# Softmax attention: one transposed head copied on ScalarE between two exponentials, one head divided on GpSimd

## The reference, cut to what matters

```
q, k = rope(q), rope(k)
dots = einsum('bhqd,bhkd->bhqk', q, k) * SCALE
attn = softmax(dots, axis=-1)
out  = einsum('bhqk,bhkd->bhqd', attn, v) @ w_out
```

## Time and profile before

| what | value |
|---|---|
| median of the runs | 1453.45 us |
| the profiled execution's own time | 1453.37 us |
| its span | 1451.5 us |
| busy share of the span: TensorE (matmul), VectorE, ScalarE, GpSimd | 90%, 71%, 54%, 36% |
| granted TensorE clock, mean of the span | 0.938 |
| share of the chain that ended last: TensorE, VectorE, "issue", ScalarE, GpSimd | 60%, 16%, 9%, 9%, 4% |

### The profile page before, as it was taken

How to read it: one execution, slowest core, us unless ns; L and a number is a source line. 1 busy time by engine, 2 the same in 40 slices (tenths; PEclk the granted TensorE clock), 3 DMA queues, 4 the chain that set the end, 5 groups by cost and what they waited for, 6 DMA issues and landing times.

```text
span 1451.5 us, 30211 instructions
## 1 busy us (share of the span) xinstructions
PE 1308.4 (90%) x9370; PEld 982.7 (68%) x9370; DVE 1025.2 (71%) x2849; ACT 785.3 (54%) x2420; POOL 520.9 (36%) x697
## 2 busy tenths in 40 slices
PE   4999999978888887699999999999999996799997
PEld 2777777753444343577777777777777775799997
DVE  5555555546887788677777777777787764688886
ACT  2232333312223222398888888888888886444442
POOL 3221211123455456544444434444444431111111
PEclk9999999978787777799999999999999998899999
DMA  8000000000000000000000000000000000000000
GB/s 255 1 1 1 0 0 0 0 1 1 1 0 0 0 0 0 1 1 2 2 1 2 1 0 0 0 0 0 0 0 0 1 1 1 1 8 14 11 11 16
DMA packets 14270, 12.22 MB, mean 8 GB/s; under 512 B 1764, under 2 KB 12536, under 8 KB 13944
## 3 DMA queue, kind: packets, MB, share of 16 engines
q1 hardware_dynamic: 14200, 11.33, 2.6%
HBM read 9.23 MB, written 2.10 MB: 8 GB/s over the span
## 4 chain that ended last, share of the span: by engine, by line
PE 60%; DVE 16%; issue 9%; ACT 9%; POOL 4%; DVEq 0%; ACTq 0%; POOLq 0%
PE bank L757 10%; PE bank L939 9%; PE bank L167 8%; PE bank L528 7%; PE bank L477 6%; PE bank L1019 6%; ACT work L956 5%; PE bank L1032 5%; DVE work L948 3%; PE bank L990 3%; ACT work L976 2%; DVE work L1187 1%; DVE work L1179 1%; POOL rstd L342 1%; DVE moe_work L777 1%
## 5 line engine op out<-in xcount | busy, mean ns | idle before, releaser
L956 ACT ACTIVATE work<-bank,work 128x256 f32<-128x256 f32 x512 | 234.8, 485 | 70.6 <-DVE work L948 70.6
L948 DVE TENSOR_REDUCE work<-bank 128x2 f32<-128x512 f32 x256 | 159.0, 684 | 133.3 <-PE bank L939 133.3
L757 PE MATMUL bank<-WrT,xT 128*128 128x512 f32 x256 | 165.0, 792 | 34.1 <-DVE moe_work L777 33.6
L922 POOL TENSOR_TENSOR work<-work 128x512 f32<-128x512 f32 x128 | 160.6, 1277 | 89.0 <-DVE work L912 89.0
L340 POOL TENSOR_SCALAR ve<-mv 128x2 f32<-128x2 f32 x128 | 29.3, 229 | 409.6 <-DVE mv L278 409.6
L976 ACT ACTIVATE work<-work 128x256 f32<-128x256 f32 x384 | 161.4, 534 | 0.0
L970 POOL TENSOR_TENSOR work<-work 128x512 f32<-128x512 f32 x64 | 66.7, 1042 | 252.6 <-DVE work L964 252.6
L486 DVE TENSOR_TENSOR la_work<-bank,tri 128x512 f32<-128x512 f32 x128 | 87.8, 686 | 84.4 <-PE bank L477 84.3
L939 PE MATMUL bank<-work 32*128 32x256 f32 x2048 | 130.4, 391 | 14.2 <-ACT XnT L372 9.8
L990 PE MATMUL bank<-ident,work 128*128 128x128 f32 x1024 | 139.4, 280 | 0.6 <-ACT work L998 0.6
L1019 PE MATMUL bank<-work 128*64 128x256 f32 x1024 | 127.3, 390 | 14.0 <-DVE work L1005 14.0
(11 more groups left out here) (166 smaller groups left out, 2890.1 us busy)
## 6 DMA issues: line engine op xcount, KB each, us to landing
X<-in_x SPq DMA_DIRECT2D x4, 512.0 KB, 5.8
wF<-in_L_ffn_h_w SPq DMA_DIRECT2D x2, 1024.0 KB, 9.6
out<-X SPq DMA_DIRECT2D x16, 128.0 KB, 1.8
w_qkv<-in_L_attn_w_qkv SPq DMA_DIRECT2D x1, 1536.0 KB, 9.4
WrT<-in_L_ffn_Wr SPq DMA_DIRECT2D x1, 1024.0 KB
w_out<-in_L_attn_w_out SPq DMA_DIRECT2D x1, 512.0 KB, 10.5
wF<-in_L_ffn_w_w SPq DMA_DIRECT2D x2, 256.0 KB, 10.3
rope_sin<-in_rope_sin SPq DMA_DIRECT2D x1, 256.0 KB
```

The lines of the kernel that those rows point to most:

```text
L757: ins = nc.tensor.matmul(unit_bank(p, b, t)[:, :], xT[:, p, t * P:(t + 1) * P], WrT[:, b * BLK:(b + 1) * BLK], start=True, stop=True)
L922: nc.gpsimd.tensor_tensor((QT if kind == "q" else KT)[:, p, a, :], rc[:, ru % 2, :], rs_[:, ru % 2, :], ALU.add).then_inc(c_rope, 1)
L948: nc.vector.tensor_reduce(nmax[:, QUAD * a + j, :], SB_[j][:, :].rearrange("p (t k) -> p t k", t=T), AX.X, ALU.max, negate=True).then_inc( ...
L956: ins = nc.scalar.activation(pr[:, a % 2, j, t, :], SB_[j][:, t * LEN:(t + 1) * LEN], ACT.Exp, bias=nmax[:, h, t:t + 1], accum_out=psum_[: ...
```

## The change

ScalarE copies the transposed head 2 of the quad before, between exponentials 0 and 1 of a slot; VectorE copies head 3 alone. The division of head 1 moves from ScalarE to GpSimd, behind that of head 0. The semaphore counts follow. After the last slot ScalarE copies head 2 and VectorE head 3.

```diff
         def sa_turn_tensor(pe, i, a, j):
             n = i * QUADS + a
-            pe.wait_ge(c_pn if j == 0 else c_pna, n + 1 if j == 0 else (QUAD - 1) * n + j)
-            if j < 2:
-                pe.wait_ge(c_ptv, reached(2 * (n - 1) + j + 1))
+            pe.wait_ge(c_pn if j < 2 else c_pna, 2 * n + j % 2 + 1)
+            if j == 1:
+                pe.wait_ge(c_ptv, reached(n))
             else:
-                pe.wait_ge(c_pta, 2 * n + j - 1)
+                pe.wait_ge(c_pta, reached(3 * n + max(j - 1, 0)))
...
         def sa_turn_scalar(act, i, a, j):
-            act.wait_ge(c_v, reached(2 * (n - 1) + 1))
+            act.wait_ge(c_v, reached(2 * (n - 1) + j // 2 + 1))
...
         def sa_pv_tensor(pe, i, p, a, k):
-            pe.wait_ge(c_pta if k == 0 else c_ptv, 2 * n + 2)
+            pe.wait_ge(c_pta, 3 * n + 2 + k)
+            if k == 1:
+                pe.wait_ge(c_ptv, n + 1)
...
@@ gpsimd, sa_step
-                    sa_norm_pool(pool, i, a, 0)
+                    for j in range(2):
+                        sa_norm_pool(pool, i, a, j)
...
@@ vector, sa_step
                     if last:
-                        for j in range(2, 4):
-                            sa_turn_vector(dve, last[0], last[2], j)
+                        sa_turn_vector(dve, last[0], last[2], 3)
...
@@ vector, after the steps
-            for j in range(2, 4):
-                sa_turn_vector(dve, SEQS - 1, QUADS - 1, j)
+            sa_turn_vector(dve, SEQS - 1, QUADS - 1, 3)
...
@@ scalar, sa_step
                     for j in range(QUAD):
                         sa_exp_scalar(act, i, a, j)
-                    for j in range(1, 4):
+                        if j == 0 and last:
+                            sa_turn_scalar(act, last[0], last[2], 2)
+                    for j in range(2, 4):
                         sa_norm_scalar(act, i, a, j)
...
@@ scalar, after the steps
+            sa_turn_scalar(act, SEQS - 1, QUADS - 1, 2)
             sa_pv_scalar(act, SEQS - 1, 1, QUADS - 1)
...
@@ tensor, before the feed-forward network
-            pe.wait_ge(c_pta, 2 * QUADS * SEQS)
-            pe.wait_ge(c_ptv, 2 * QUADS * SEQS)
+            pe.wait_ge(c_pta, 3 * QUADS * SEQS)
+            pe.wait_ge(c_ptv, QUADS * SEQS)
```

## The result

The changed kernel takes 1473.52 us (median of 4 runs, 1472.39 to 1473.96) where the kernel before takes 1453.14 us on the same chip: a ratio of 1.0138, 95% interval 1.012 to 1.0156. It is 20 us slower. The forecast was 1470.5, in a range of 1463 to 1479.

A forecast was written before the change was run, and what follows sets the result against it. TensorE sets the pace, k's start bound by exponential 1. Quads 1 and 2 +14.4, quad 0 +5.2, quad 3 +1.0 and −2.2, sequence 15 −1.2: +17.2 us on 1453.37, forecast 1470.5, range 1463 to 1479.

The forecast's parts named there:

- The copy's price: ScalarE, ahead of exponential 1: copying head 2 delays exponentials 1 to 3 and the k projection by 0.48 us.
- The lower and upper bounds: ScalarE's copy of head 2: at least 0.45 us (pace of half an exponential head), at most 0.61 (no overlap).
- VectorE's saving eaten by exponential 3: VectorE: one copy fewer saves 0.60 us, but the second reciprocals wait for exponential 3, so ropes end 0.25 later.
- the loop's first kind of quad 0: Five loop sequences whose scores after quad 0 wait 0.3 us for L914: +0.25 us each.
- The division costs nothing on GpSimd: GpSimd's second L970, 1.04 us for head 1, ends before the transposes that need it: cost nothing.
- signs of being wrong: k still 0.92 us behind q, transposes waiting for L970's second instruction, or the clock falling in the loop.
- Quad 3: End of quad 3: L372 and the scores come about 0.2 us earlier in eleven slots, −2.2 us.
- Sequence 15: Last sequence, without k projection: −0.12 us a slot, ScalarE's 0.36 once, −0.5 at the end; together −1.2 us.
- The clock: TensorE's clock stays at 1.00; rival: it falls once a sequence, +30 us, 1500 (chance 0.05 together with late GpSimd division).
- sequence 0: The four slots of the first sequence: forecast +1.4 us.
- Faster: Rival: the copy fits in a gap between exponential 1 and k, only the relief remains, −6 us, 1447.5; chance 0.04.
- No change: Rival: TensorE, its work unchanged, absorbs the delay in the waits after quads 0 and 3: 1453 us; chance 0.03.

The follow-up runs named there:

- Experiment 3: The changed kernel with ScalarE's copy of head 2 behind exponential 1 instead of exponential 0: 1457.80 us.
- experiments 6 and 7: First half of P times V moved ahead of the q projection, in the kernel before (1445.34 us) and in the changed kernel (1451.55 us).
- experiment 2: The changed kernel with the division of head 1 back on ScalarE, the copy staying between exponentials 0 and 1: 1481.23 us.
- experiment 1: The kernel before with only the division of head 1 moved from ScalarE to GpSimd: 1447.71 us.
- Experiment 5: The changed kernel with GpSimd dividing heads 0 and 2 and ScalarE heads 1 and 3: 1469.53 us.
- experiment 4: The changed kernel with the first half of P times V moved between the q and k projections on TensorE: 1463.04 us.

## Why the prediction was right, point by point

- **The copy's price, and where it is paid.** Forecast 0.48 us a slot, from the pace of two L998; measured 0.48, with k 1.40 behind q. The lower and upper bounds weren't needed. The Trainium skill, "ScalarE: Activation LUTs", gives an overlap of about 93 ns between neighbours; the copy of 0.59 us at a pace of 0.48 overlaps by 0.11, so the rows of the trace were the better source by a few hundredths. Experiment 3 shows that in quads 1 and 2 the place costs and not the instruction; experiments 6 and 7, with 284.5 us for these quads without the copy and with it, show that this cost exists only as long as TensorE has nothing else to do at that point.
- **VectorE's saving eaten by exponential 3.** Forecast L914 0.25 later in the loop's first kind of quad 0, quad 0 +5.2 us in all; measured +5.1. After the change VectorE waits 0.42 us for exponential 3 ahead of the second reciprocal. Its line in the changed kernel stands in experiment 2. Experiments 3 and 7 leave this term as it is, 128.6 us.
- **The division costs nothing on GpSimd.** Right (experiment 1). One of my signs of being wrong was that L970 would be named as what transposes wait for, and it is: over the whole span the changed kernel's L990 has 4.3 us in 10 waits of the weight loads, and 0.8 us in 2 waits of the matmuls, both in slot 0. The sign was set too fine. Slot 0 takes 10.30 us in experiment 2, without the second division on GpSimd, and 10.31 in experiment 3, with it.
- **Quad 3: the step that failed.** I wrote that ScalarE ends its part of a slot 0.36 us earlier, since it sheds two L976 (0.84) for a copy (0.48). The sum was right and the conclusion wrong: L372 ended at 9.22 us into the slot instead of 9.16, and TensorE waits for it behind its transposes of heads 0 and 1, as its last step before the scores. I had costed the removed division by its duration and had not asked what it covered. Head 1's division was the one whose reciprocals were there early; its 0.84 us hid the second reciprocal. Without it ScalarE stands idle. The rows give it to the hundredth. Before, the first L976 starts at 908.93 in a slot that begins at 902.56, 6.37 us in; after, at 921.47 − 914.23 = 7.24. Of these 0.87 us the copy is 0.48 and the wait 0.39 (0.24 of it shows as idle time; in the rest, it seems, the overlap with the read ahead of it is lost). From L976 to L372 it is 923.09 − 921.47 = 1.62 instead of 2.39, so shedding two gave 0.77 and not 0.84, and L372 itself is 0.04 shorter. 0.48 + 0.39 − 0.77 − 0.04 = +0.06, which is what L372 moved. Experiment 1 shows the wait without the copy too, 0.33 us of it idle. The expected −2.2 us became +0.9 over the 13 sequences. Experiment 5 takes the wait away and gets back 3.0 us in quad 3. The wait for L372 did shrink, to 0.4 us by name and 4.3 us more under "issue", where I had forecast below 4. But it shrank by TensorE's later transposes alone and not by the 0.2 us that L372 was to gain.
- **Sequence 15: near by luck.** Forecast −1.2, measured −0.9, but 0.76 of it is the clock in one slot. The forecast's own parts were −0.12 in each of three slots (measured +0.03 and −0.14 in the two others) and −0.86 at the end, of which nothing shows: from the start of the last scores to the end of the span it is 226.7 us before and after.
- **The clock.** From 625 us to the last sequence it stayed at 1.00, with 0.42 us more idle time at one place. In the last sequence it fell after the long wait as before, at moments that differ, which took about 0.8 us off the difference of the two profiled executions. The first slot, 10.30 us before and 10.05 after, differs by its clock as well (0.75 and 0.87 between 600 and 625 us); that is the 0.3 us by which sequence 0 misses its forecast.
- **Rivals.** "Faster" needed slack between exponential 1 and k, and there was 0.05 us of it. "No change" needed waits that could absorb the delay of k, and quads 1 and 2 have none behind k. The Trainium skill, "Perfetto Trace Analysis", section on the most-contended engine, says to optimize the engine with the highest occupancy first. Taken alone, that gives no price to a shift between the other engines: TensorE's busy time hardly changed (1308.4 and 1309.7 us), and the time rose by 20 us.

## What to carry to other kernels

Before work is put into a queue, ask who waits for the very next instruction there: 0.48 us of work on an engine that idles 1.0 us a slot cost 0.48 us of the slot, as the idle time stood in another place. When work is taken out of a queue, ask what wait it was covering, and take the piece that has to wait, not the one that is ready (head 2 and not head 1). And where the bound engine waits between two pieces in a fixed order, look for a ready piece to put there: ahead of q it was worth 7.5 us, and 19.2 together with the better division.

## What the hardware showed that I had not expected

Splitting P times V into two halves of 8 matmuls costs 1.01 to 1.02 us a half, where 16 in a row go on to the next group in 1.87 to 1.88: about 0.15 us more. The run doesn't tell what costs it; the two groups differ from their neighbours in operands and tile shape, and no run varies these one at a time. I had taken the order of TensorE's groups to be free, and was 3 us low for it in experiment 4.

The scores that wait for L372 don't start right at its end. In sequences 2 and 14, which are written out, they start 0.05 us behind it (9.16 to 9.21 us into the slot in the kernel before). In the loop's first sequence it is 0.33 us in nearly every slot and every run in which L372 binds (9.16 to 9.49, 9.22 to 9.55, 8.81 to 9.14), and in the loop's second sequence, behind which TensorE's stream goes back to the start of the loop, 0.7 to 0.9. No run shows why a wait inside the loop costs more.
